# Weighing the turned states by diagonal matrices of C in a selective scan

## The chip, the cores and the metric

The kernel runs on one core of a Trainium2 chip. The metric is the device time of one execution in microseconds (us), taken as the median of repeated runs. A profile of one execution gives the time of every instruction.

## The reference

The reference is a small perceiver in float32 over 16 batches of 64 tokens with 256 channels (1024 tokens): a cross attention over 1601 context rows, a Mamba layer, a spiking feed-forward layer, a second cross attention, a self attention with a phase term, and a mixture of eight experts. The change touches the Mamba layer, whose core is this recurrence over the 64 tokens `l` of each batch (512 inner channels `d`, 16 states `n`):

```python
deltaA = jnp.exp(jnp.einsum('bld,dn->bldn', delta, a))
deltaBu = jnp.einsum('bld,bln,bld->bldn', delta, b, u)
def step(h, inp):
    dA_t, dBu_t, c_t = inp
    h = dA_t * h + dBu_t
    y = jnp.einsum('bdn,bn->bd', h, c_t)
    return (h, y)
```

The output of the scan plus `D * u` is gated by `silu(z)` and projected back to 256 channels.

## The kernel before

The Mamba stage is `mamba` (L694). Channels stand on the 128 partitions and tokens along the free axis, so the 512 channels are four blocks `c` and the 1024 tokens are two halves of 512. A unit is one token half and two channel blocks; there are four units (`UNITS`), each with 16 states, so the scan has 64 steps `s`. One step handles 128 partitions x 1024 elements (two blocks `j` of 512 tokens). Every engine runs its own list in program order, and the engines meet through semaphores. For step `s`:

- GpSimd (POOL) multiplies `du` (step size times input) by row B of state n, copied to all partitions by a transfer (`bs`, two states per transfer, three slots), into `dbu` (L847). There are three `dbu` buffers, so the product of step s waits for the scan of step s-3.
- ScalarE (ACT) makes the decays exp(-A delta) in PSUM with two instructions (`decays`, L965); it does this two steps ahead, in two buffers.
- VectorE (DVE) runs the recurrence over all 1024 elements with one scan instruction (`scan`, L1095), into three buffers `S`.
- TensorE (PE) turns the states with eight 128x128 transposes into the PSUM tile `T` (`turn`, L1174), in two halves b of four, so that tokens stand on partitions.
- The turned states are multiplied by C. Tokens are on partitions, so C is one number per partition, a column of the tile `CT`: four pieces `q` of 128x256, on ACT (`weigh`, L976), of which the last piece of 34 of the 64 steps is done by DVE (`on_dve`, L1105).
- PE turns the products back and adds them up in the PSUM tile `Y` (`add`, L1188): eight transposes against the identity.

PE's list in the loop is turn(s), then add(s-1); turn(s) waits for the scan of s and for `T` to have been emptied of step s-1. In units 1 to 3 four extra matmuls put `D * u` into `Y` (`share_of_input`, L1158). After 16 steps a unit is complete: DVE multiplies `Y` by the gate in two instructions (`gate`, L1119), which stand in DVE's list behind scan(s+1) and before scan(s+2), and PE's next add waits for them. The output projection (L1195) begins after add 62.

SyncE (SP) issues the transfers in a list of its own: late weights, the row copies of B to DRAM (`b_rows`), the `bs` loads of the first six states, then one `bs` load for every two steps, each behind a wait for POOL (L806).

Four products `du = delta * u` for the second token half are POOL's too, in front of steps 18, 22, 26 and 30 (`steps_by_input`, L826). Ahead of the loop PE turns the rows of C into `CT` (L1256) and DVE copies them (L1088).

Of the kernel before, what the change touches and what calls it, by code (L numbers as in the profile page):

```python
# [6 lines left out]
F32 = mybir.dt.float32  # L7
# [114 lines left out]
def cross_attention(nc, k, first_loads, columns, constants, loads):  # L122
# [3 lines left out]
    with ExitStack() as ctx:  # L126
# [28 lines left out]
        s_q0 = sem("a_q0")  # L155
# [370 lines left out]
        def _(e):  # L526
# [41 lines left out]
            def key_bias(f):  # L568

                ts, xs, turned = ((range(0, 1), prob[0][:, 0:D], 1), (range(1, TILES - 1), prob[1][:, 0:(TILES - 2) * D], 5),  # L570
                                  (range(TILES - 1, TILES), on[:, :], 5))[f]
                n, at = len(ts), slice(ts[0], ts[-1] + 1)
                xs = xs.rearrange("p (t d) -> p t d", d=D)
                if f == 0:
                    e.wait_ge(s_fold, 4)
                    e.tensor_copy(qconst, X[:, D:D + 1]).then_inc(s_qr, 1)
                e.wait_ge(s_t0, turned)
                e.tensor_tensor(xs, xs, X[:, 0:D].unsqueeze(1).to_broadcast([P, n, D]), ALU.mult).then_inc(s_qr, 1)
                e.wait_ge(s_qr, 2 * f + 2)
                e.reduce_sum(qraw[:, at], xs, AX.X).then_inc(s_qr, 1)  # L580
                e.wait_ge(s_qr, 2 * f + 3)
                e.tensor_scalar(qbk[:, at], qraw[:, at], qconst, scale, ALU.add, ALU.mult).then_inc(s_q0, 1)
# [9 lines left out]
            def maximum(i):  # L592
                e.wait_ge(s_sc, i + 1)
                e.reduce_max(mx[:, :], S[:, 0:LK], AX.X).then_inc(s_m1, 1)  # L594
                e.wait_ge(s_m1, i * 2 + 1)
                e.wait_ge(s_q0, 1 if i == 0 else 2 if i < TILES - 1 else 3)
# [96 lines left out]

def mamba(nc, k, m, loads):  # L694
# [11 lines left out]
    with ExitStack() as ctx:  # L706
# [4 lines left out]
        weighed = [sb(f"weighed{i}", [P, 4 * Q]) for i in range(2)]  # L711
        CT = sb("CT", [P, TILES, 2 * DS])
# [5 lines left out]
        acc4 = [weighed[r // 2][:, r % 2 * HALF:(r % 2 + 1) * HALF].rearrange("p (b l) -> p b l", l=L) for r in range(4)]  # L718
# [3 lines left out]
        qT = weighed[0][:, 0:HALF]  # L722
        kTb = k.xz[:, :, :].rearrange("p c n -> p (c n)")[:, 0:KD * (D + 1)].rearrange("p (c n) -> p c n", c=KD)
        qk, qk_at = Y.rearrange("p (j n) -> p j n", j=KD), HALF // 2 + 8
        vT, bvT = weighed[1][:, 0:HALF], weighed[1][:, HALF:HALF + KD]
# [24 lines left out]
        s_e0 = sem("n_e0")  # L750
        s_e1 = sem("n_e1")
        s_q = sem("n_q")
# [9 lines left out]
                    ("xj", 1), ("in", 12), ("dt", 1), ("in", 13), ("in", 14), ("in", 15), ("wT", 0), ("wT", 1), ("CT", 0),  # L762
# [20 lines left out]
        def on_dve(s):  # L783

            return s > 1 and s % 16 in (0, 1, 3, 5, 7, 9, 11, 13, 15)

        def dve_before(s):
            return sum(on_dve(i) for i in range(s))

        def c_of(s, q):  # L790
            return CT[:, 4 * UNITS[s // DS][0] + q, DS + s % DS:DS + s % DS + 1]

        @block.sync
        def _(e):
            loads(e)
            for h in range(2):
                if h == 0:
                    e.wait_ge(s_fa, ac_at["row", 0])
                else:
                    e.wait_ge(s_xe, 1)  # L800
                e.dma_start(m.b_dram[h], m.rows[B_AT:B_AT + DS, h * HALF:(h + 1) * HALF]).then_inc(s_bd, 16)
                e.wait_ge(s_bd, 16 * (h + 1))
                if h == 0:
                    for g in range(SLOTS):
                        load_states(e, m, g)
            for g in range(SLOTS, STEPS // 2):  # L806
                e.wait_ge(s_bu, 2 * (g - SLOTS) + 2)
                load_states(e, m, g)

        @block.gpsimd  # L810
        def _(e):
            def add_parts(c):

                e.wait_ge(s_fa, ac_at["ln", c // 2])
                e.wait_ge(s_rz, FIRST_POSITIVE.index(c) + 1)
# [3 lines left out]
            def steps_by_input(h, c):  # L819

                if h:
                    e.wait_ge(s_dl, CH)
                else:
                    e.wait_ge(s_dup, (1, 2, 5, 6)[c])
                hs = slice(h * HALF, (h + 1) * HALF)
                e.tensor_tensor(m.du[:, c, hs], m.delta[:, c, hs], m.u[:, c, hs], ALU.mult).then_inc(s_dup, 1)  # L826
# [3 lines left out]
            for c in range(2):  # L830
                steps_by_input(0, c)
            for s in range(STEPS):
                if s == 1:
                    add_parts(2)
                    add_parts(3)
                if s in (6, 10):
                    steps_by_input(0, 2 + (s - 6) // 4)
# [19 lines left out]
        def _(e):  # L857
# [145 lines left out]
            e.wait_ge(s_ct, 1)  # L1003
            for s in range(STEPS):
# [4 lines left out]
                for b in (1, 0) if on_dve(s) else (0, 1):  # L1009
                    weigh(s, b)  # L1010
# [7 lines left out]
        def _(e):  # L1018
# [68 lines left out]
            e.tensor_copy(bvT, spare[:, 0:KD])  # L1087
            e.tensor_copy(CT[:, :, :], T[:, 0:TILES * 2 * DS].rearrange("p (t n) -> p t n", n=2 * DS)).then_inc(s_ct, 1)  # L1088

# [7 lines left out]

            def weigh(s):

                e.wait_ge(s_ct, 1)  # L1100
                e.wait_ge(s_t, 2 * s + 2)
                e.wait_ge(s_e1, s + 1)
                if s >= 2:
                    e.wait_ge(s_y, 2 * (s - 2) + 2)
                e.tensor_scalar(weighed[s % 2][:, 3 * Q:4 * Q], T[:, 3 * Q:4 * Q], c_of(s, 3), None, ALU.mult  # L1105
                                ).then_inc(s_q, 1)
# [13 lines left out]

            scan(0)
# [30 lines left out]
        def _(e):  # L1152
# [9 lines left out]
            def turn(s, b):  # L1162
                if b == 0:
                    e.wait_ge(s_h, s + 1)
                    e.wait_ge(s_e0, s)
# [3 lines left out]
                else:  # L1169
                    e.wait_ge(s_e1, s)  # L1170
                    e.wait_ge(s_q, dve_before(s))
# [93 lines left out]
            e.wait_ge(s_fp, pe_at["CT", 0])  # L1265
# [1839 lines left out]
def perceiver(nc, t, out):  # L3105
    with ExitStack() as ctx:
# [9 lines left out]
        k.b_dram = nc.dram_tensor("b_rows", (2, DS, HALF), F32, kind="Internal").ap()  # L3116
        k.trig = sb("trig", [P, 2, DH])
# [14 lines left out]
        k.s_wz = sem("s_wz")  # L3132
# [13 lines left out]
        k.n_ident = k.n_const = 5 + 3 + 3 + E  # L3146
# [22 lines left out]
        def early_loads(e):  # L3169
# [10 lines left out]
            e.wait_ge(k.s_wz, 1)  # L3180
# [27 lines left out]
        def constants(e):  # L3208
# [28 lines left out]
            e.memset(k.wfq[:, :], 0.0).then_inc(k.s_wz, 1)  # L3237
# [42 lines left out]
        with ExitStack() as mctx:  # L3280
# [8 lines left out]
            m.s_bs = [sem(f"n_bs{i}") for i in range(SLOTS)]  # L3289
            mamba(nc, k, m, late_weights)  # L3290
# [75 lines left out]
```

## Time and profile before

| | |
|---|---|
| median of three runs | 658.33 us (658.2 to 660.86) |
| time of the profiled execution | 657.73 us |
| its span, first to last instruction | 656.0 us |
| the scan loop, first turn to last add | 199.9 to 364.5 us |
| busy in the span: PE, DVE, ACT, POOL | 92%, 71%, 56%, 36% |

The shares are an average over stages with different limits; the change concerns one stage, the scan loop, a quarter of the span. PE counts as busy from the start of a matmul to its modelled end, about 0.17 us after the next one may start, so the distance between starts and not the duration of one says what a matmul costs in a series. An ordinary float32 matmul appears as two matmul records, a transpose as one.

### The profile page before, as it was taken

Reading aid. Unit: us, or ns where it says so; the run is one execution under the profiler, and the core shown is the slowest. Engines: PE = TensorE matmul, PEld = TensorE weight load, DVE = VectorE, ACT = ScalarE, POOL = GpSimd, SP = SyncE. Lnnn points to the kernel's source line nnn. Section 1 sums busy time; section 2 is a strip of 40 time slices with the busy share of each in tenths; the row PEclk is TensorE's granted clock in tenths of the full one; section 3 lists DMA queues with packets and bytes.
Section 4 is the critical chain, followed back from the end, with each engine's and each line's share of the span. In section 5 each row is a group of like instructions: output and inputs, shape, how many; then the busy total and the mean of one; then the engine's idle time right before and its main releaser. Section 6 shows DMA issues by size and latency. Waiting matters only on the chain. (4 is left out here: it accounts for less than half of the span.)

```text
span 656.0 us, 11718 instructions
## 1 busy us (share of the span) xinstructions
PE 602.4 (92%) x4436; PEld 460.0 (70%) x4436; DVE 465.2 (71%) x798; ACT 368.7 (56%) x700; POOL 235.1 (36%) x190
## 2 busy tenths in 40 slices
PE   7999999999998778878788999999999899999997
PEld 6645555464366667767677888887777768889897
DVE  2753433347767999999999517788978878886554
ACT  2311111136889999999999333344656465555343
POOL 2000000000089999999898200035651022231000
PEclk8999999999999999999999999999999999999999
DMA  9999999984903232233220000000100022210001
GB/s 335 407 415 416 416 418 414 420 324 159 258 12 107 106 104 97 97 98 126 99 97 1 1 1 17 1 0 19 36 2 2 1 65 85 61 49 1 32 1 33
DMA packets 32831, 87.52 MB, mean 133 GB/s; under 512 B 8092, under 2 KB 20840, under 8 KB 30600
## 3 DMA queue, kind: packets, MB, share of 16 engines
q1 hardware_dynamic: 32088, 86.18, 35.7%
q8 instruction: 36, 0.59, 0.4%
q10 hardware_dynamic: 688, 0.59, 0.3%
q14 instruction: 19, 0.16, 0.1%
HBM read 84.53 MB, written 1.11 MB: 131 GB/s over the span
## 5 line engine op out<-in xcount | busy, mean ns | idle before, releaser
L847 POOL TENSOR_TENSOR dbu<-du,bs 128x1024 f32<-128x1024 f32 x64 | 149.8, 2365 | 7.0 <-DVE w_in L1095 4.6
L976 ACT ACTIVATE weighed<-T,CT 128x256 f32<-128x256 f32 x222 | 94.9, 592 | 1.2 <-PE T L1174 0.9
L1095 DVE TENSOR_TENSOR_SCAN w_in<-hS,dbu 128x1024 f32<-128x1024 f32 x42 | 94.6, 2271 | 0.4 <-ACT hS L965 0.4
L965 ACT ACTIVATE hS<-delta,negA 128x504 f32<-128x504 f32 x128 | 90.7, 813 | 5.3 <-DVE xn L1095 2.5
L1188 PE MATMUL Y<-ident,weighed 128*128 128x128 f32 x512 | 66.8, 273 | 0.1
L1174 PE MATMUL T<-ident,w_in 128*128 128x128 f32 x336 | 45.9, 279 | 19.8 <-ACT weighed L976 13.8
L1188 PEld LDWEIGHTS Y<-ident,weighed 128*128 128x128 f32 x512 | 57.8, 141 | 0.9 <-DVE sres L1119 0.3
L1174 PEld LDWEIGHTS T<-ident,w_in 128*128 128x128 f32 x336 | 36.1, 140 | 30.7 <-DVE w_in L1095 27.4
L1095 DVE TENSOR_TENSOR_SCAN xn<-hS,dbu 128x1024 f32<-128x1024 f32 x22 | 50.0, 2274 | 2.3 <-ACT hS L965 2.3
L425 POOL COPY w_xp<-w_xp 128x64 f32<-128x64 f32 x3 | 0.6, 234 | 138.8 <-DMA w_out<-in_w_out 138.8
L314 PE MATMUL O<-cN,pT 123*64 123x256 f32 (+1 forms) x384 | 46.7, 385 | 3.8 <-DMA cN<-in_ctx 3.1
L452 ACT ACTIVATE prob<-S,nbias 128x1601 f32<-128x1601 f32 x8 | 12.8, 1597 | 58.9 <-DVE nbias L601 58.9
L300 PE MATMUL S<-cT,qkT 128*64 128x512 f32 (+1 forms) x256 | 44.8, 502 | 0.9 <-DMA cT<-in_ctxT 0.7
L2784 ACT ACTIVATE hid<-BK,cols 128x512 f32<-128x512 f32 x32 | 22.0, 689 | 38.1 <-PE BK L2616 37.0
L3028 DVE TENSOR_TENSOR h_lo<-hid,h_hi 128x512 fp32r<-128x512 f32 x32 | 22.1, 693 | 28.6 <-ACT h_hi L2784 28.6
L314 PEld LDWEIGHTS O<-cN,pT 123*64 123x64 f32 (+1 forms) x384 | 25.4, 136 | 18.9 <-DMA cN<-in_ctx 5.0
L300 PEld LDWEIGHTS S<-cT,qkT 128*64 128x64 f32 x256 | 16.3, 136 | 30.1 <-issue 28.1
L2590 PE MATMUL BK<-w_hi,h_hi 128*128 128x256 f32 x128 | 37.1, 290 | 0.1
L594 DVE TENSOR_REDUCE mx<-S 128x1 f32<-128x1601 f32 x8 | 14.6, 1824 | 31.6 <-PE S L300 31.6
L2847 POOL TENSOR_TENSOR w_lo<-raw_w,w_hi 128x512 fp32r<-128x512 f32 x14 | 18.0, 1299 | 52.9 <-ACT w_hi L2727 52.9
L2590 PE MATMUL BK<-w_lo,h_hi 128*128 128x256 f32 x128 | 36.2, 283 | 0.0
L2590 PE MATMUL BK<-w_hi,h_lo 128*128 128x256 f32 x128 | 36.2, 283 | 0.0
(444 smaller groups left out, 1340.7 us busy)
## 6 DMA issues: line engine op xcount, KB each, us to landing
cN<-in_ctx SPq DMA_DIRECT2D x8, 3072.0 KB, 24.3
cT<-in_ctxT SPq DMA_DIRECT2D x7, 3202.0 KB, 24.5
bs<-b_rows SPq DMA_DIRECT2D x32, 512.0 KB, 3.7
raw_w<-in_w SPq DMA_DIRECT2D x16, 256.0 KB, 3.0
cT<-in_ctxT SPq DMA_DIRECT2D x1, 2178.0 KB, 12.2
cR<-in_ctx SPq DMA_DIRECT2D x8, 256.0 KB, 23.7
w<-in_w SPq DMA_DIRECT2D x7, 256.0 KB, 7.9
vs<-vx SPq DMA_DIRECT2D x8, 136.0 KB, 2.4
```

The costliest lines, as they stand in the source:

```text
L300: j = e.matmul(S[64 * b:64 * b + 64, c * HALF:c * HALF + w], qkT[:, kt, q:q + 64], cT[r][:, b, kt, c * HALF:c * HALF + w], start=kt == 0, ...
L314: j = e.matmul(O[64 * b:64 * b + 64, 0:D], pT[0:n_keys(c), c, 64 * b:64 * b + 64], v, start=c == 0, stop=c == ROWS)
L847: e.tensor_tensor(dbu[s % NB][:, :, :], half(m.du, s // DS), row, ALU.mult).then_inc(s_bu, 1)
L965: i = e.activation(by_batch(A[s % 2][:, j * HALF:(j + 1) * HALF]), by_batch(m.delta[:, c, h * HALF:(h + 1) * HALF]), ACT.Exp, scale=m.negA ...
L976: i = e.activation(weighed[s % 2][:, q * Q:(q + 1) * Q], T[:, q * Q:(q + 1) * Q], ACT.Copy, scale=c_of(s, q))
L1095: e.tensor_tensor_scan(S[s % NS], A[s % 2][:, :], dbu[s % NB][:, :, :].rearrange("p c n -> p (c n)"), 0.0, ALU.mult, ALU.add).then_inc(s_h, 1)
L1174: i = e.transpose(T[:, q * Q + j * P:q * Q + (j + 1) * P], S[s % NS][:, j * HALF + q * P:j * HALF + (q + 1) * P], k.ident[:, :])
L1188: i = e.matmul(Y[:, j * HALF + q * P:j * HALF + (q + 1) * P], weighed[s % 2][:, q * Q + j * P:q * Q + (j + 1) * P], k.ident[:, :], start=u ...
L2590: ins = e.matmul(dst, a, b, start=first and i == 0, stop=last and i == 2)
L2784: i = e.activation(dst, HB[m][:, :], ACT.Relu, bias=col(k, "b1", 2 * x + m))
L2847: e.tensor_tensor(k.w_lo[j // 2][:, j % 2, :, :], k.raw[j % SLOTS_W][:, :, :], k.w_hi[j // 2][:, j % 2, :, :].bitcast(F32), ALU.subtract). ...
L3028: e.tensor_tensor(h_lo[n % 2][:, m, :], hid[m][:, :], h_hi[n % 2][:, m, :].bitcast(F32), ALU.subtract).then_inc(s_l, 1)
```

## The change

Weighing by C moves from ACT and DVE to PE. ACT now only copies the turned states out of PSUM (two copies of 128x512 per step, `keep_turned`), DVE's part of it is gone, and `add` becomes a real float32 matmul: the copied states are the stationary operand and, in place of the identity, the moving operand is a diagonal matrix with C of that state and those 128 tokens on its diagonal. `CT`, its transposes and its copy are gone.

The diagonal matrices come from DRAM. For each token half, SP clears a 4 MB buffer from a zeroed tile, writes the 8192 values of C onto the diagonals with four transfers of 2048 elements of 4 bytes each, and loads 512 KB (two states, 128 x 2 x 512) for every two steps into three slots (`xT` halves and `xz`). For the first half all of that stands before the loop; for the second half the clearing is spread over the loop's groups 6 to 9 and the writing stands in group 12. SP's list is now, for each group g of two steps: wait and load `bs` of g; what is left of the second half's clearing or writing; wait and load the diagonals of g-1.

The four second-half products of step size and input move from POOL to DVE, behind the scans issued at steps 18, 23, 34 and 39. The two semaphores of the evacuation become one: turn(s, b) waits for copy b of step s-1, as before in substance. A few waits on constants are merged (`s_q0` into `s_qr`, `s_wz` into `s_const`).

```diff
+def clear_diagonals(e, m, h, a=0, n=DS):
+    e.dma_start(m.c_dram[h, a:a + n, 0:P * HALF].rearrange("n (p q) -> p n q", p=P),
+                m.blank.unsqueeze(1).to_broadcast([P, n, HALF])).then_inc(m.s_cd, 16)
+
+def write_diagonals(e, m, h):
+    for b in range(HALF // P):
+        diagonal = m.c_dram[h, :, b * P:b * P + P * (HALF + 1)].rearrange("n (t x) -> n t x", x=HALF + 1)[:, :, 0]
+        e.dma_start(diagonal, m.rows[C_AT:C_AT + DS, h * HALF + b * P:h * HALF + (b + 1) * P],
+                    allow_slow_non_contiguous=True).then_inc(m.s_cd, 16)
+
+def load_diagonals(e, m, g):
+    h = UNITS[2 * g // DS][0]
+    n = 2 * g % DS
+    e.dma_start(m.cd[g % SLOTS][:, :, :], m.c_dram[h, n:n + 2, 0:P * HALF].rearrange("n (p q) -> p n q", p=P)
+                ).then_inc(m.s_cl[g % SLOTS], 16)
...
@@ SyncE @@
             loads(e)
+            e.wait_ge(k.s_const, k.n_const + 1)
+            clear_diagonals(e, m, 0)
             for h in range(2):
...
                 if h == 0:
                     for g in range(SLOTS):
                         load_states(e, m, g)
-            for g in range(SLOTS, STEPS // 2):
-                e.wait_ge(s_bu, 2 * (g - SLOTS) + 2)
-                load_states(e, m, g)
+                    e.wait_ge(m.s_cd, 16)
+                    write_diagonals(e, m, 0)
+            e.wait_ge(m.s_cd, 16 * 5)
+            e.wait_ge(s_fp, pe_at["in", 15])
+            for g in range(SLOTS):
+                if g == SLOTS - 1:
+                    e.wait_ge(s_fp, pe_at["b", 0])
+                load_diagonals(e, m, g)
+            for g in range(SLOTS, STEPS // 2 + 1):
+                if g < STEPS // 2:
+                    e.wait_ge(s_bu, 2 * (g - SLOTS) + 2)
+                    load_states(e, m, g)
+                if g in range(6, 10):
+                    clear_diagonals(e, m, 1, 4 * (g - 6), 4)
+                if g == 12:
+                    e.wait_ge(m.s_cd, 16 * 9)
+                    write_diagonals(e, m, 1)
+                if g == DS + 1:
+                    e.wait_ge(m.s_cd, 16 * 13)
+                if g > SLOTS:
+                    e.wait_ge(s_y, 4 * (g - 1 - SLOTS) + 4)
+                    load_diagonals(e, m, g - 1)
...
@@ GpSimd @@
+            e.memset(m.blank, 0.0).then_inc(k.s_const, 1)
...
-                if s in (18, 22, 26, 30):
-                    steps_by_input(1, (18, 22, 26, 30).index(s))
...
@@ ScalarE @@
-            def weigh(s, b):
+            def keep_turned(s, b):
                 e.wait_ge(s_t, 2 * s + b + 1)
                 if s >= 2:
                     e.wait_ge(s_y, 2 * (s - 2) + b + 1)
-                for q in (2 * b, 2 * b + 1):
-                    if q < 3 or not on_dve(s):
-                        i = e.activation(weighed[s % 2][:, q * Q:(q + 1) * Q], T[:, q * Q:(q + 1) * Q], ACT.Copy,
-                                         scale=c_of(s, q))
-                i.then_inc((s_e0, s_e1)[b], 1)
+                e.activation(turned[s % 2][:, b * HALF:(b + 1) * HALF], T[:, b * HALF:(b + 1) * HALF], ACT.Copy
+                             ).then_inc(s_e, 1)
...
@@ VectorE @@
-            def weigh(s):
...
+            def steps_by_input(c):
+                e.wait_ge(s_dl, CH)
+                hs = slice(HALF, 2 * HALF)
+                e.tensor_tensor(m.du[:, c, hs], m.delta[:, c, hs], m.u[:, c, hs], ALU.mult).then_inc(s_dup, 1)
...
-                if on_dve(s):
-                    weigh(s)
+                if s in (18, 23, 34, 39):
+                    steps_by_input((18, 23, 34, 39).index(s))
...
@@ TensorE @@
             def add(s, b):
                 u, n = divmod(s, DS)
-                e.wait_ge((s_e0, s_e1)[b], s + 1)
-                if b and on_dve(s):
-                    e.wait_ge(s_q, dve_before(s + 1))
+                e.wait_ge(s_e, 2 * s + b + 1)
+                if b == 0:
+                    e.wait_ge(m.s_cl[s // 2 % SLOTS], 16 * (s // 2 // SLOTS + 1))
                 for j in range(2):
                     if u and n == 0 and b == 0:
                         e.wait_ge(s_yg, 2 * (u - 1) + j + 1)
                     for q in (2 * b, 2 * b + 1):
                         i = e.matmul(Y[:, j * HALF + q * P:j * HALF + (q + 1) * P],
-                                     weighed[s % 2][:, q * Q + j * P:q * Q + (j + 1) * P], k.ident[:, :],
-                                     start=u > 0 and n == 0 and q == 0, stop=True, is_transpose=True, skip_group_check=True)
+                                     turned[s % 2][:, q * Q + j * P:q * Q + (j + 1) * P],
+                                     m.cd[s // 2 % SLOTS][:, s % 2, q * P:(q + 1) * P],
+                                     start=u > 0 and n == 0 and q == 0, stop=True, skip_group_check=True)
                 i.then_inc(s_y, 1)
...
-            e.wait_ge(s_rg, 3)
-            for t in range(TILES):
-                i = e.transpose(T[:, t * 2 * DS:(t + 1) * 2 * DS], m.rows[32:64, t * P:(t + 1) * P], k.ident[32:64, 32:64])
-            i.then_inc(s_fp, 1)
```

## Rows read from the trace of the kernel before

**Rows 1.** Busy time per stretch; columns PE, PEld, DVE, ACT, POOL, clock, DMA share, GB/s

```profile
199.80:364.50 164.70, 134.17 (x1061) 116.32 (x1062) 154.41 (x102) 159.95 (x350) 154.78 (x70) 1.00 0.27 90
```

**Rows 2.** Groups of instructions by line, from 199.8 to 364.5 us

```profile
L847 POOL TENSOR_TENSOR dbu<-du,bs 128x1024 f32<-128x1024 f32 x61 | 142.8, 2365 | 6.9 <-DVE w_in L1095 4.6 <-DVE xn L1095 2.1
L976 ACT ACTIVATE weighed<-T,CT 128x256 f32<-128x256 f32 x222 | 94.9, 592 | 1.2 <-PE T L1174 0.9
L1095 DVE TENSOR_TENSOR_SCAN w_in<-hS,dbu 128x1024 f32<-128x1024 f32 x41 | 92.4, 2272 | 0.4 <-ACT hS L965 0.4
...
L1188 PE MATMUL Y<-ident,weighed 128*128 128x128 f32 x512 | 66.8, 273 | 0.1
...
L1105 DVE TENSOR_SCALAR weighed<-T,CT 128x256 f32<-128x256 f32 x34 | 16.2, 477 | 5.7 <-PE Y L1188 3.3 <-issue 0.5
...
L826 POOL TENSOR_TENSOR du<-delta,u 128x512 f32<-128x512 f32 x6 | 7.7, 1276 | 0.0
```

**Rows 3.** What ended PE's idle time before its turns (line L1174): us, times

```profile
  DVE w_in L1095: 33.9, 43
  ACT weighed L976: 22.2, 33
```

**Rows 4.** Instructions in time: turn and add of one step, then a gate

```profile
280.88 1.07 PE L1174 MATMUL T<-ident,w_in 128*128 128x128 f32 x8 [0.86 <-ACT weighed L976]
...
281.79 1.04 PE L1188 MATMUL Y<-ident,weighed 128*128 128x128 f32 x8
...
283.19 1.28 DVE L1119 TENSOR_TENSOR sres<-Y,sres 128x512 f32<-128x512 f32 x2
```

**Rows 5.** PE in time: a float32 product with 128 columns, elsewhere in the kernel

```profile
22.04 1.06 PE L273 MATMUL ptp<-xT,wq 128*128 128x128 f32 x8
```

**Rows 6.** In time: first add, two shares of input, output projection, last add

```profile
203.36 1.04 PE L1188 MATMUL Y<-ident,weighed 128*128 128x128 f32 x8
...
354.35 0.60 PE L1158 MATMUL Y<-u,diagD 128*128 128x256 f32 x2
...
361.69 1.89 PE L1195 MATMUL hS<-w_out,sres 128*128 128x256 f32 x8
...
363.42 1.04 PE L1188 MATMUL Y<-ident,weighed 128*128 128x128 f32 x8
```

**Rows 7.** In time: ACT from PSUM at 512 columns, DVE at 512, ACT's decays

```profile
173.23 2.42 ACT L896 ACTIVATE delta<-hS,cols 128x512 f32<-128x512 f32 x4
...
191.38 2.55 DVE L1051 TENSOR_TENSOR delta<-hS,delta 128x512 f32<-128x512 f32 x4 [0.40 <-ACT delta L907]
...
193.38 2.50 ACT L965 ACTIVATE hS<-delta,negA 128x504 f32<-128x504 f32 x4 [0.58 <-DVE hS L1078]
```

**Rows 8.** The page: GB/s in 40 slices of the span

```profile
GB/s 335 407 415 416 416 418 414 420 324 159 258 12 107 106 104 97 97 98 126 99 97 1 1 1 17 1 0 19 36 2 2 1 65 85 61 49 1 32 1 33
```

**Rows 9.** DMA from 168.4 to 174.2 us: the 4096 pieces of c0T, 256 bytes each

```profile
DMA packets 4248, 1.15 MB, mean 199 GB/s; under 512 B 4162, under 2 KB 4232, under 8 KB 4248
```

**Rows 10.** DMA from 183.4 to 184.1 us: the b_rows copy to DRAM

```profile
DMA packets 32, 0.03 MB, mean 47 GB/s; under 512 B 16, under 2 KB 16, under 8 KB 32
## 3 DMA queue, kind: packets, MB, share of 16 engines
q1 hardware_dynamic: 32, 0.03, 21.0%
```

**Rows 11.** The page, DMA issues: KB each, median us from issue to landing

```profile
bs<-b_rows SPq DMA_DIRECT2D x32, 512.0 KB, 3.7
...
b_rows<-xn SPq DMA_DIRECT2D x2, 32.0 KB, 2.6
```

**Rows 12.** Busy time per stretch at the kernel's start; the seventh column is PE's clock

```profile
6.00:9.40 3.40, 1.55 (x15) 1.31 (x14) 1.20 (x5) 0.52 (x1) 0.00 (x0) 1.00 1.06 391
9.40:12.80 3.40, 3.40 (x12) 2.86 (x12) 1.67 (x8) 0.73 (x4) 0.00 (x0) 0.50 1.03 411
```

More of the change, by code:

```diff
@@ L578, in key_bias @@
                 e.tensor_tensor(xs, xs, X[:, 0:D].unsqueeze(1).to_broadcast([P, n, D]), ALU.mult).then_inc(s_qr, 1)
-                e.wait_ge(s_qr, 2 * f + 2)
+                e.wait_ge(s_qr, 3 * f + 2)
                 e.reduce_sum(qraw[:, at], xs, AX.X).then_inc(s_qr, 1)
-                e.wait_ge(s_qr, 2 * f + 3)
-                e.tensor_scalar(qbk[:, at], qraw[:, at], qconst, scale, ALU.add, ALU.mult).then_inc(s_q0, 1)
+                e.wait_ge(s_qr, 3 * f + 3)
+                e.tensor_scalar(qbk[:, at], qraw[:, at], qconst, scale, ALU.add, ALU.mult).then_inc(s_qr, 1)
             def evacuate(i, g):
@@ L595, in maximum @@
                 e.wait_ge(s_m1, i * 2 + 1)
-                e.wait_ge(s_q0, 1 if i == 0 else 2 if i < TILES - 1 else 3)
+                e.wait_ge(s_qr, 4 if i == 0 else 7 if i < TILES - 1 else 10)
                 e.tensor_scalar(full_max[:, :], mx[:, :], scale, qbk[:, i:i + 1], ALU.mult, ALU.add
@@ L710, in mamba @@
         dbu = [sb(f"dbu{i}", [P, 2, HALF]) for i in range(NB)]
-        weighed = [sb(f"weighed{i}", [P, 4 * Q]) for i in range(2)]
-        CT = sb("CT", [P, TILES, 2 * DS])
+        turned = [sb(f"turned{i}", [P, 4 * Q]) for i in range(2)]
         S = [k.xn[:, 4:8, :].rearrange("p t d -> p (t d)")] + [k.w_in[:, i, :] for i in range(2)]
@@ L717, in mamba @@
         T = ps("T", [P, 2 * HALF])
-        acc4 = [weighed[r // 2][:, r % 2 * HALF:(r % 2 + 1) * HALF].rearrange("p (b l) -> p b l", l=L) for r in range(4)]
+        acc4 = [turned[r // 2][:, r % 2 * HALF:(r % 2 + 1) * HALF].rearrange("p (b l) -> p b l", l=L) for r in range(4)]
         expA = sb("expA", [P, CH * DS])
@@ L749, in mamba @@
         s_t = sem("n_t")
-        s_e0 = sem("n_e0")
-        s_e1 = sem("n_e1")
-        s_q = sem("n_q")
+        s_e = sem("n_e")
         s_y = sem("n_y")
@@ L781, in half @@
             return a[:, 2 * cp:2 * cp + 2, h * HALF:(h + 1) * HALF]
[L783 to L791, printed above, removed]
         @block.sync
@@ L817, in add_parts @@
                 e.tensor_tensor(m.delta[:, c, hs], m.delta[:, c, hs], m.du[:, c, hs], ALU.add).then_inc(s_dup, 1)
[L819 to L825, printed above, removed]
+            def steps_by_input(c):
+                e.wait_ge(s_dup, (1, 2, 5, 6)[c])
+                hs = slice(0, HALF)
                 e.tensor_tensor(m.du[:, c, hs], m.delta[:, c, hs], m.u[:, c, hs], ALU.mult).then_inc(s_dup, 1)
@@ L830, in _ @@
             for c in range(2):
-                steps_by_input(0, c)
+                steps_by_input(c)
             for s in range(STEPS):
@@ L836, in _ @@
                 if s in (6, 10):
-                    steps_by_input(0, 2 + (s - 6) // 4)
-                if s in (18, 22, 26, 30):
-                    steps_by_input(1, (18, 22, 26, 30).index(s))
+                    steps_by_input(2 + (s - 6) // 4)
                 if s % DS == 0:
@@ L1008, in _ @@
                     e.preload_act_table_set("silu_and_others")
-                for b in (1, 0) if on_dve(s) else (0, 1):
-                    weigh(s, b)
+                for b in range(2):
+                    keep_turned(s, b)
                 if s == STEPS - 2:
@@ L1086, in _ @@
             e.wait_ge(s_fp, pe_at["bv", 0])
-            e.tensor_copy(bvT, spare[:, 0:KD])
-            e.tensor_copy(CT[:, :, :], T[:, 0:TILES * 2 * DS].rearrange("p (t n) -> p t n", n=2 * DS)).then_inc(s_ct, 1)
+            e.tensor_copy(bvT, spare[:, 0:KD]).then_inc(s_ct, 1)
             def scan(s):
@@ L1168, in turn @@
                         e.wait_ge(s_vo, 2)
-                else:
-                    e.wait_ge(s_e1, s)
-                    e.wait_ge(s_q, dve_before(s))
+                if s:
+                    e.wait_ge(s_e, 2 * s - 1 + b)
                 for q in (2 * b, 2 * b + 1):
@@ L1264, in _ @@
             i.then_inc(s_fp, 1)
-            e.wait_ge(s_fp, pe_at["CT", 0])
+            e.wait_ge(s_rg, 3)
             for c in range(KD):
@@ L3116, in perceiver @@
         k.b_dram = nc.dram_tensor("b_rows", (2, DS, HALF), F32, kind="Internal").ap()
+        k.c_dram = nc.dram_tensor("c_diagonals", (2, DS, (P + 1) * HALF), F32, kind="Internal").ap()
         k.trig = sb("trig", [P, 2, DH])
@@ L3145, in perceiver @@
         k.s_d0 = sem("s_d0")
-        k.n_ident = k.n_const = 5 + 3 + 3 + E
+        k.n_const = 5 + 3 + 3 + E + 1
         k.n_w0 = 48
@@ L3179, in early_loads @@
             e.dma_start(k.trig[:, :, :], t["trig"]).then_inc(k.s_w4, 16)
-            e.wait_ge(k.s_wz, 1)
+            e.wait_ge(k.s_const, k.n_const)
             e.dma_start(k.wfq[1:3, :], t["wfq"]).then_inc(k.s_w5, 16)
@@ L3236, in constants @@
                 chain(e.memset(k.iota8[:, i:i + 1], float(i)))
-            e.memset(k.wfq[:, :], 0.0).then_inc(k.s_wz, 1)
+            chain(e.memset(k.wfq[:, :], 0.0))
         cross_attention(nc, k, first_loads, columns, constants, early_loads)
@@ L3289, in perceiver @@
             m.s_bs = [sem(f"n_bs{i}") for i in range(SLOTS)]
+            m.c_dram = k.c_dram
+            m.cd = [k.xT[:, i, :].rearrange("p (n t) -> p n t", n=2) for i in range(KD)] + [k.xz]
+            m.blank = k.gated[:, 0, :]
+            m.s_cd = sem("n_cd")
+            m.s_cl = [sem(f"n_cl{i}") for i in range(SLOTS)]
             mamba(nc, k, m, late_weights)
```

18 lines of the change are left out of this document (4 added, 14 removed).

## The prediction, made before the result

> **What bounds the kernel now.** I read the busy time of the scan stage first, then its groups by line, then what ended PE's idle time, and last single steps in order of time. The stage table says that between 199.8 and 364.5 us PE is busy for 134.2 of 164.7 us, and ACT (160.0), POOL (154.8) and DVE (154.4) more than that [rows 1]. So three engines are nearly full there and PE is the one with room. The groups give the prices: a scan 2.27 us on DVE, a product of B 2.365 us on POOL, DVE's part of the weighing 34 times 0.477 [rows 2]. A step takes 164.7 / 64 = 2.57 us. PE's idle time before its turns ends with a scan (33.9 us in 43 waits, plus those of the third scan buffer) or with a weighing by ACT (22.2 us in 33) [rows 3]: PE waits for both of the engines that the change relieves. That is what speaks for it.
>
> **PE's own price of a step.** A turn has eight records in 1.07 us and an add eight in 1.04, and the add starts 0.91 us after the turn, so there is no gap between them [rows 4]. The last record of a series stands for 0.273 us [rows 2], so starts are (1.04 - 0.273) / 7 = 0.110 us apart, and eight cost 0.877. Turn and add are 1.75 us of a step of 2.57.
>
> The change makes the add an ordinary float32 product with 128 columns. There is one like it in the trace: four products of 128x128 by 128x128 in the projection of the queries are eight records in 1.06 us [rows 5], which gives (1.06 - 0.275) / 7 = 0.112 us from start to start. The price of one record is that of a transpose; but there are two to a product. An add becomes 16 records, 1.79 us, 0.91 more than before. Nothing else in PE's loop changes, and a step then costs PE 0.877 + 1.79 = 2.67 us against a step of 2.57 now. This is the step on which the forecast hangs: the engine with room gets more than its room.
>
> **The sum for the loop.** I count from the first add (203.36) to the start of the output projection behind add 62 (361.69) [rows 6]: 158.3 us. PE's new work in that stretch: 63 adds x 1.79 = 112.6; 62 turns x 0.877 = 54.3; 12 products for the share of the input, two records each, 0.60 - 0.38 = 0.22 apart [rows 6], 5.2. Together 172.1, **+13.8 us** with no wait at all.
>
> The other engines stay below 2.67 a step. ACT: two decays, (2.50 - 0.68) / 3 = 0.61 each, and two copies of 512 columns from PSUM, (2.42 - 0.69) / 3 = 0.58 each [rows 7], 2.37. POOL: 64 x 2.365, and 2.5 for two products and 2.5 for two sums left to it [rows 2], 156.4 in all, 2.44 a step. DVE: 64 x 2.27, six gates and four products at 0.64 [rows 4, 7], 152, 2.38 a step. The move of the four products (5.1 us off POOL at 1.276 each [rows 2], 2.6 us onto DVE) and DVE's 16 us of weighing cost and give nothing, since PE hides both; without PE in the way they would give what the first rival says.
>
> **Unit boundaries.** When a unit is complete the two gates take 1.28 us [rows 4] and stand in DVE's list before the next scan. In a loop in which PE sets the pace they can't start before the last add ends, at a moment x; PE has meanwhile one turn (0.88). The gates run from x+0.2 to x+1.5, the second half of the first add waits until then, about 0.3; the scan behind the gates runs from x+1.5 to x+3.8, while PE is through with turn and add at x+3.0: a further 0.9. That is 1.2 at each of three boundaries, **+3.5**. The bounds are 0 (if the scans have run further ahead than their three buffers suggest) and 6. The product of DVE at step 18 finds the scans back to 0.3 ahead by then and costs nothing.
>
> **The tail.** Behind add 62 the projection's first part, 8 x 0.217 = 1.7, and the last add until now took 361.69 to 364.3 [rows 6], 2.6; the last add will be 1.8: 3.5, **+0.9**. The turns of C that go ahead of the loop are eight short ones beside work of ACT; I give them nothing (0 to -0.6).
>
> **The start.** The first add now also waits for the first diagonals, behind a chain on SP and the DMA queues. The small pieces of c0T are on the queues until 174.2 us [rows 9]. Behind them come 4 MB of zeros to DRAM. At the best rate of the page (415 GB/s [rows 8]) that is 10.1 us. The one write to DRAM of such pieces (2 KB) occupied the engines for 21.0% of 0.7 us for 16 pieces, one on each engine, 0.147 us a piece [rows 10], which would make 128 x 0.147 = 18.8 us. I take 14: 188.2. The copy of B's rows lies behind on the same queue and lands about 190, then three `bs` loads (3.7 us to landing [rows 11]): POOL's first product starts at about 193.5, a few us later, which the scans still bear, because the first add comes later still.
>
> Then C is written: 4 x 2048 pieces of 4 bytes, 128 of each transfer on an engine. The trace has no write of this kind. From below: the pieces of 256 bytes of c0T, 4162 small ones in 5.8 us on 16 engines [rows 9], 0.022 us each. From above: 0.147, the whole 2 KB piece to DRAM. I take 0.022, since the number of pieces and not their bytes is what the two have in common: 4 x 128 x 0.022 = 11.3 us behind the `bs` loads (drained about 194.5), so 205.8. SP waits for the landing (1.5 more) and loads the first diagonals (3.7 [rows 11], like a `bs` load in size): 211 with these, 207 with the faster clearing; I take 210. The first add starts at 210 instead of 203.4: **+6.6**. Queued on SP behind that: the `bs` load of steps 6 and 7, which POOL wants only when scan 3 is through; it lands near 212 and is hidden by PE's delay.
>
> During that wait PE stands still for 6 us. At the kernel's start PE was busy for 1.55 of 3.4 us and in the next 3.4 us had a clock of 0.50, 1.2 GHz [rows 12]. The same after this wait costs half of 3.4: **+1.5**, bounds 0 and 3. The Trainium skill (TensorE: Matmul & The Clock Gate, Part 1) states that idleness brings the clock down to half; these rows agree.
>
> The second half's C is written from group 12, in the loop. SP comes to it when add 15 is done, and stays until the load of the diagonals for step 22 can follow: 0.6 + 11.3 + 3.7, and 2.6 for the loads ahead, 18.2 us. PE needs them after seven turns, six adds, a boundary and four share products: 6.1 + 10.7 + 1.2 + 0.9 = 18.9. Hidden, with less than a us to spare. The clearings (1 MB in groups 6 to 9) and the loads (512 KB a group more) take the DMA share from 0.27 [rows 1] to some 0.6 in the loop, hidden behind 5.3 us a group.
>
> **Sum.** 13.8 + 3.5 + 0.9 + 6.6 + 1.5 = 26.3 us. The profiled execution took 657.73 (span 656.0), 0.6 below the median: 684 from it, 684.6 from the median. I say **684.5**.
>
> **Rivals.** *First, the other side: PE keeps its cover.* If an add with a diagonal costs PE no more than eight records (0.88), POOL sets the pace, with 156.4 us from its first product at 193.5 to 350; the last scan ends at 352.2, and a turn and an add later (354) the projection starts, against 361.69 now [rows 6]: 7.6 less, 651 us. It decides once an add takes less than about (158.3 - 54.3 - 5.2 - 3.5) / 63 = 1.51 us, with no wait at the start. For it speaks that ACT, DVE and POOL are all relieved; against it the eight records for four products [rows 5]. 4%.
>
> *Second, the diagonal writes are slow.* Each 0.01 us more for a piece is 5.1 us at the start and, once the 0.7 us of slack are gone, 5.1 in the loop. At 0.05: 14.3 + 13.6, 712. At the upper bound of 0.147: 64 + 63, near 811. Against it speaks only that the trace's small pieces are cheap, and they are reads from DRAM; for it that DRAM writes of 2 KB took 0.147. The Trainium skill (DMA: Bandwidth & Descriptors, Specifications) states that below 512 bytes the DMA engine reads, modifies and writes; it gives no time per piece, and no run here shows one. 30%.
>
> *Third, no wait at the start.* With faster clearing and pieces of 0.015, the diagonals land near 203: 13.8 + 3.5 + 0.9, 677. It is part of my own case, its lower half.
>
> *Fourth, no change.* The loop's extra work would have to be covered by PE waits that I count too low; the slack is 158.3 - (63 + 62) x 0.877 - 5.2 = 43.5 us and the addition 63 x 0.91 = 57.3. 3%.
>
> **Numbers.** My case (672 to 693) 63%, slow writes 30%, no change 3%, faster 4%. The range goes from 672 (no start wait, half the boundary cost) to 720 (pieces of about 0.058): it leaves out 7% below and some 11% above; my case's own range is 672 to 693. A measurement of this kernel tells 0.5% (3.3 us) from no change: faster 0.04, same 0.03, slower 0.93.
>
> **What would show it.** L1188's successor: 1024 records with starts 0.112 apart, 1.8 us an add; PE's idle time in the loop before turns nearly gone but for three places at steps 18, 34 and 50 (scan behind the gates); ACT idle 0.3 us a step, waiting for PE; POOL and DVE waiting for buffers. First add near 210, waiting for a DMA; steps then 2.67 us apart. A step below 2.5 proves the PE price wrong; a first add beyond 215, or a wait for a DMA at step 22, shows the second rival. What I trust least is the 4-byte write.

## The result, and the profile after

The changed kernel takes **695.31 us** (691.54 to 696.48, four runs), the kernel before 658.97 in the same runs: a ratio of 1.054 with an interval of 1.049 to 1.059, or 36.3 us more. The forecast was 684.5, with a range of 672 to 720. The profiled execution took 696.03, its span is 694.2 against 656.0.

The page of the changed kernel, engines first (busy us, share of the span, instructions), then two of its groups that answer to [rows 2]:

```profile
PE 655.3 (94%) x4940; PEld 526.7 (76%) x4940; DVE 457.2 (66%) x767; ACT 354.8 (51%) x606; POOL 232.8 (34%) x187
...
L1203 PE MATMUL Y<-xT,turned 128*128 128x128 f32 x704 | 87.9, 279 | 11.4 <-DMA xT<-c_diagonals 11.4
...
L1203 PE MATMUL Y<-xz,turned 128*128 128x128 f32 x320 | 40.7, 282 | 3.0 <-DMA xz<-c_diagonals 3.0
```

The add is line 1203 now, with 704 + 320 = 1024 records in place of 512. The stretches of the scan loop (busy PE, PEld, DVE, ACT, POOL, then PE's clock, DMA share, GB/s), which answer to [rows 1]:

```profile
206.20:214.70 8.50, 0.00 (x0) 0.00 (x1) 1.29 (x1) 0.00 (x0) 0.09 (x1) 0.50 0.31 109
214.70:219.80 5.10, 5.07 (x24) 5.10 (x25) 0.00 (x0) 0.43 (x1) 0.57 (x1) 0.51 0.96 335
219.80:256.40 36.60, 36.60 (x332) 36.60 (x331) 29.78 (x13) 31.30 (x56) 33.11 (x15) 1.00 0.84 296
256.40:280.90 24.50, 20.90 (x180) 20.07 (x179) 20.25 (x12) 18.16 (x33) 14.95 (x7) 1.00 0.91 120
280.90:285.30 4.40, 4.39 (x25) 4.40 (x26) 0.43 (x1) 0.26 (x1) 2.87 (x2) 0.61 1.04 408
285.30:397.40 112.10, 110.91 (x974) 109.09 (x973) 89.92 (x44) 89.92 (x159) 94.05 (x40) 1.00 0.46 163
```

Where PE has its data and its clock it is busy without a break (36.60 of 36.60 us), and DVE, ACT and POOL have become the engines with room. Before the first add it stands still for 11.4 us (8.5 of them in this table), then works at a clock of 0.51 (about 1.2 GHz of 2.4); a second, smaller hole lies before 280.9, with a clock of 0.61 behind it. The timeline of PE (start, length, instruction, and in brackets what it waited for): the first wait, two steps of the steady loop, the second wait, and the end of the loop:

```profile
214.73 3.75 PE L1203 MATMUL Y<-xT,turned 128*128 128x128 f32 x16 [11.43 <-DMA xT<-c_diagonals]
...
226.97 1.04 PE L1189 MATMUL T<-ident,w_in 128*128 128x128 f32 x8
...
227.84 1.95 PE L1203 MATMUL Y<-xz,turned 128*128 128x128 f32 x16
...
229.63 1.04 PE L1189 MATMUL T<-ident,xn 128*128 128x128 f32 x8
...
280.91 3.52 PE L1203 MATMUL Y<-xz,turned 128*128 128x128 f32 x16 [3.02 <-DMA xz<-c_diagonals]
...
397.42 1.89 PE L1211 MATMUL hS<-w_out,sres 128*128 128x256 f32 x8
...
399.15 1.95 PE L1203 MATMUL Y<-xT,turned 128*128 128x128 f32 x16
```

A step is 229.63 - 226.97 = 2.66 us; the 16 records of an add start (1.95 - 0.275) / 15 = 0.112 us apart. The first add starts at 214.73 against 203.36 [rows 6], 11.4 us later, and from there to the projection it is 182.7 us against 158.3, 24.4 more. From the starts of the adds, one by one, these 24.4 are: the PE records 13.6; three unit boundaries of 1.13 (steps of 2.82 and 3.63 in place of 2.66), 3.4; step 1, which takes 5.13 at the low clock, 2.5; steps 22 and 23 (6.28 and 4.37; in the kernel without the second writing, below, 3.10 and 2.66), 4.9. Of these 4.9, about 3.2 are the wait for diagonals (step 22) and 1.7 are the lower clock behind it (step 23, in which the add takes 3.52 us instead of 1.95). The last add costs 0.9 more. That leaves 1.5 of the 38.2 us of span, behind the loop, whose work is unchanged. It says nothing of the change: from the end of the last add to the end, the thirteen executions at hand take between 291.4 and 293.1 us, whatever the kernel (the kernel before 291.5, the changed kernel 293.1, the last run below 293.0).

### The profile page after: what moved, and what is told of

It reads as the page before. It is cut to its first block and busy times, and to the rows that moved or that the text cites. A ratio compares the mean times of both kernels' runs of the same rounds, so it can differ in the third digit from the quotient of the medians.

```text
span 694.2 us, 12538 instructions
## 1 busy us (share of the span) xinstructions
PE 655.3 (94%) x4940; PEld 526.7 (76%) x4940; DVE 457.2 (66%) x767; ACT 354.8 (51%) x606; POOL 232.8 (34%) x187
## 5 line engine op out<-in xcount | busy, mean ns | idle before, releaser
L1116 DVE TENSOR_TENSOR_SCAN w_in<-hS,dbu 128x1024 f32<-128x1024 f32 x42 | 95.4, 2281 | 30.0 <-ACT hS L991 24.4
L1203 PE MATMUL Y<-xT,turned 128*128 128x128 f32 x704 | 87.9, 279 | 11.4 <-DMA xT<-c_diagonals 11.4
L1203 PEld LDWEIGHTS Y<-xT,turned 128*128 128x128 f32 x704 | 83.9, 195 | 12.1 <-issue 12.1
L1000 ACT ACTIVATE turned<-T 128x512 f32<-128x512 f32 x128 | 69.4, 593 | 45.7 <-PE T L1189 45.6
L991 ACT ACTIVATE hS<-delta,negA 128x504 f32<-128x504 f32 x128 | 82.6, 685 | 9.3 <-DVE w_in L1116 4.8
L1189 PE MATMUL T<-ident,w_in 128*128 128x128 f32 x336 | 44.4, 276 | 1.2 <-DVE w_in L1116 1.2
L1203 PE MATMUL Y<-xz,turned 128*128 128x128 f32 x320 | 40.7, 282 | 3.0 <-DMA xz<-c_diagonals 3.0
L1203 PEld LDWEIGHTS Y<-xz,turned 128*128 128x128 f32 x320 | 38.8, 198 | 3.5 <-issue 3.4
L1189 PEld LDWEIGHTS T<-ident,w_in 128*128 128x128 f32 x336 | 39.1, 143 | 2.9 <-DVE w_in L1116 1.6
## 6 DMA issues: line engine op xcount, KB each, us to landing
c_diagonals<-gated SPq DMA_DIRECT2D x1, 4096.0 KB, 14.2
```

What stands on the lines that cost most here:

```text
L991: i = e.activation(by_batch(A[s % 2][:, j * HALF:(j + 1) * HALF]), by_batch(m.delta[:, c, h * HALF:(h + 1) * HALF]), ACT.Exp, scale=m.negA ...
L1000: e.activation(turned[s % 2][:, b * HALF:(b + 1) * HALF], T[:, b * HALF:(b + 1) * HALF], ACT.Copy).then_inc(s_e, 1)
L1116: e.tensor_tensor_scan(S[s % NS], A[s % 2][:, :], dbu[s % NB][:, :, :].rearrange("p c n -> p (c n)"), 0.0, ALU.mult, ALU.add).then_inc(s_h, 1)
L1189: i = e.transpose(T[:, q * Q + j * P:q * Q + (j + 1) * P], S[s % NS][:, j * HALF + q * P:j * HALF + (q + 1) * P], k.ident[:, :])
```

## The experiments

Theory A: PE's 16 records set the pace of the loop from the first add to the last, so what starts late is paid in full; the waits for diagonals at the start and at step 22 are queueing, and come on top. Theory B: the transfers, their order on SP and their traffic slow the loop, and the records would be hidden.

**Without the first writing (e1).**

```diff
-                    write_diagonals(e, m, 0)
```

(the counts of the waits behind it are adapted).

> The four transfers that write C of the first token half onto the diagonals are left out (these diagonals stay zero, so the first half lacks its scan part); clearing and loading stay. Changed kernel: first add at 214.8 us, step 1 takes 5.1 us, all later steps 2.66. Theory A (PE sets the pace from the first add on, so every late start is paid in full): the first diagonals land near 195, the first add moves to about 203.3 and the clock does not fall: 11.4 + 2.5 us less, 681.5 (679 to 684). Theory B (the engines behind would catch up, the start is not additive): no less than 690.

Measured: 677.42 us, ratio 1.029 (1.025 to 1.033), below the range expected. The first add moves to where it was before the change, and step 1 takes 2.66:

```profile
203.36 1.95 PE L1201 MATMUL Y<-xT,turned 128*128 128x128 f32 x16
205.15 1.04 PE L1187 MATMUL T<-ident,w_in 128*128 128x128 f32 x8
```

Theory A holds for the start. The gain is 4 us more than expected: steps 22 and 23 are down to 3.95 and 2.73 from 6.28 and 4.37, with the clock at 1.00. The second writing's pieces pass in 10.5 us in both executions, but the load behind them lands 18.5 us after SP came to the writing here (10.4 from its issue), and 20.8 us in the changed kernel (12.3 from its issue), while PE wants it after 17.9 in both. So that wait is an edge: 2.3 us on the queue decide whether PE stands still and loses its clock. Why the load landed sooner here was not found.

**Without the second writing (e2).**

```diff
-                    write_diagonals(e, m, 1)
```

(with its place in the waits).

> The four transfers in group 12 that write the second half's C are left out (the second half lacks its scan part). In the changed kernel steps 22 and 23 take 6.3 and 4.4 us in place of 2.66. Theory A (these two are waits for diagonals queued behind the writing): 5.3 us less, 690 (689 to 691.5), and steps 22 and 23 at 2.66. Theory B (they are contention of loads, not the writing): steps 22 and 23 stay long, 695.

Measured: 687.77 us, ratio 1.044 (1.042 to 1.046). Steps 22 and 23 are 3.10 (with its share of input) and 2.66: the long steps were the writing's. The total is 2 us below what was expected, just outside the range. The profiled execution shows a reason: its first add came at 211.8 instead of 214.7, and step 1 took 4.10 in place of 5.13. The first writing, the same code in both, took about 14.5 us here and 16 there; what makes it vary is not known.

**Adds as transposes, all transfers kept (e3).**

```diff
-                                     m.cd[s // 2 % SLOTS][:, s % 2, q * P:(q + 1) * P],
-                                     start=u > 0 and n == 0 and q == 0, stop=True, skip_group_check=True)
+                                     k.ident[:, :],
+                                     start=u > 0 and n == 0 and q == 0, stop=True, is_transpose=True, skip_group_check=True)
```

> The adds are transposes against the identity again (8 records), all transfers, waits and the other edits stay; nothing is weighed by C. Theory A (PE's 16 records per add are what sets the loop): first add still at 214.8, then steps near 2.4 to 2.45 set by POOL and ACT, scans made ahead are used up first: 664 (659 to 670). Theory B (the transfers, SP's order and the memory traffic slow the loop): over 680, with waits for bs or diagonals all along.

Measured: 663.34 us, ratio 1.007 (1.005 to 1.009). Most steps are 2.18 to 2.33 us (some are 1.75 to 1.8; steps 19 and 35 take 7.24 and 6.41, see the next run) although every transfer and wait of the change is there and the first add comes only at 212.0. Theory B is out: what makes the loop slow is the second record of each product. The transfers are not free in this kernel either: it takes 14.2 us more than the next one, which has none, 8.8 of them before the first add.

**No diagonals at all, adds as transposes (e7).**

```diff
-            clear_diagonals(e, m, 0)
...
-                    write_diagonals(e, m, 0)
...
-                load_diagonals(e, m, g)
```

(with their counterparts in the loop and the waits for them; the adds are changed as in the run before).

> No clearing, no writing, no loading of diagonals, adds as transposes; ACT's two plain copies and the four products on DVE stay; nothing is weighed by C. This is what the relief of ACT, DVE and POOL is worth when PE has its cover (my first rival, put at 651 with a late start, here the start is not late). Theory A: steps of 2.40 to 2.45, POOL the bound: 649 (646 to 653). Theory B (the loop before is bound by the handshake of PE and ACT, not by their work): 655 to 659.

Measured: 649.18 us, ratio 0.986 (0.984 to 0.989). This is the first rival's world, and its size is near what was put: 9.3 us below the kernel before, where the rival had 7.6. Most steps here are 2.18 or 2.33 long, which are the distances between DVE's scans and between POOL's products in a series; both are below the durations (2.27 and 2.365) by which I had counted. One step is 7.2 us long. POOL and DVE around it:

```profile
237.13 9.33 POOL L852 TENSOR_TENSOR dbu<-du,bs 128x1024 f32<-128x1024 f32 x4
249.34 2.38 POOL L852 TENSOR_TENSOR dbu<-du,bs 128x1024 f32<-128x1024 f32 x1 [2.89 <-DVE w_in L1095]
```

```profile
242.71 4.29 DVE L1115 TENSOR_TENSOR du<-delta,u 128x512 f32<-128x512 f32 x1
```

The moved product takes 4.29 us; the other three of this execution take 1.06 to 1.42, and the shortest of any run 0.66. It begins inside a series of POOL's products without a pause and ends at 247.00, 0.54 us after that series (246.46). The scans behind it wait, and PE with them for 4.0 us, behind which its clock is 0.51 from 249.2 to 252.6.

**The same with the four products back on POOL (e11).**

```diff
+                if s in (18, 22, 26, 30):
+                    steps_by_input((18, 22, 26, 30).index(s), 1)
...
-                if s in (18, 23, 34, 39):
-                    steps_by_input((18, 23, 34, 39).index(s))
```

> e7 (no diagonals, nothing weighed by C) with the four second-half products back on POOL, as in the kernel before. In e7 one of them took 4.29 us on DVE in place of 0.66, and the step behind it 7.2 us. Theory A (DVE's product with both operands in SBUF waits for a stretch of POOL's products to end, and all scans behind it): that step is gone, 5 us less, while POOL gets 5.1 us more of its own, which is the bound: 649 (647 to 651), no change in sum. Theory B (the move is worth POOL's 5 us, the 4.29 were hidden): 654.

Measured: 647.75 us, ratio 0.983 (0.982 to 0.985). The 7.2 us step is gone (the longest is 3.91) and POOL's own 5 us stand in its place: within 1.5 us of no change, as expected. Of this part the move gains nothing even where PE has room.

**The products on DVE in the kernel before (e6).**

```diff
-                if s in (18, 22, 26, 30):
-                    steps_by_input(1, (18, 22, 26, 30).index(s))
...
+                if s in (18, 23, 34, 39):
+                    steps_by_input((18, 23, 34, 39).index(s))
```

> The kernel before with one part of the change alone: the four second-half products of step size and input on DVE behind scans 19, 24, 35 and 40 instead of on POOL. Theory A (ACT with 160 of 164.7 us and its handshake with PE set the loop, POOL's 5 us are hidden): 658 to 660, no change. Theory B (POOL is the bound): 4 to 5 us less, 654.

Measured: 659.58 us, ratio 1.001 (1.000 to 1.003). No change to speak of: POOL alone was not the bound. That DVE waited long for the moved products does not hide a gain here, since they took only 0.66 to 0.96 us each.

**PE kept busy through the wait (e5).**

```diff
-                for q in (2 * b, 2 * b + 1):
+                for q in (2 * b, 2 * b + 1) * (26 if (s, b) == (1, 1) else 1):
```

> Turn 1's second half is done 26 times over (same values, one signal at the end), so that PE works for about 11 us of its wait for the first diagonals. Theory A (step 1 took 5.13 us and the first adds 3.3 instead of 1.67 because the clock had fallen to half in the wait): the granted clock stays at 1.00 there, first add still near 214.8, 2.5 us less: 692.8 (691.5 to 694). Theory B (the slow first steps are late diagonals or copies): 695 to 696, and the first steps as long as before.

Measured: 691.9 us, ratio 1.050 (1.047 to 1.053). The same two stretches as above, with PE at work in the first:

```profile
206.20:215.60 9.40, 8.80 (x81) 8.57 (x79) 0.00 (x0) 0.56 (x2) 1.04 (x1) 1.00 0.38 89
215.60:220.00 4.40, 4.37 (x39) 4.40 (x40) 2.29 (x1) 3.09 (x7) 0.00 (x0) 1.00 1.04 369
```

The clock stays at 1.00, with nothing but transposes on PE in the first stretch, and step 1 takes 2.73 in place of 5.13: 2.4 us, although the first add came 0.9 later. The slow first steps were the clock's. The Trainium skill (TensorE: Matmul & The Clock Gate, Part 1) has idleness bring the clock to half; the two executions agree.

**The same computation with the transfers in another order (e4).**

```diff
+            clear_diagonals(e, m, 0)
             loads(e)
-            clear_diagonals(e, m, 0)
...
-                if g in range(6, 10):
-                    clear_diagonals(e, m, 1, 4 * (g - 6), 4)
-                if g == 12:
-                    e.wait_ge(m.s_cd, 16 * 9)
-                    write_diagonals(e, m, 1)
+                if g in range(4, 8):
+                    clear_diagonals(e, m, 1, 4 * (g - 4), 4)
+                if g == 9:
+                    e.wait_ge(m.s_cd, 16 * 9)
+                if g in (9, 11, 13, 15):
+                    write_diagonals(e, m, 1, ((g - 9) // 2,))
+                if g in range(18, 26):
+                    k.later_weights(e, g - 18)
```

> Same computation as the changed kernel. The first clearing goes ahead of all other transfers of the stage, weights that only later stages need are loaded in groups 18 to 25, the second half's clearing comes in groups 4 to 7 and its writing one transfer at a time in groups 9, 11, 13, 15. Theory A (start and step 22 are pure queueing, PE's 2.66 a step remains): first add near 203, no long step: 676 (673 to 679). Theory B (the writing costs the same wherever it stands): at least 685.

Measured: 676.45 us, ratio 1.027 (1.025 to 1.029), as theory A has it to half a us. PE in the loop, 203 to 380 us, and one step:

```profile
203.00:380.00 177.00, 175.12 (x1538) 172.36 (x1537) 145.39 (x71) 143.33 (x252) 148.75 (x64) 1.00 0.73 227
```

```profile
240.94 1.95 PE L1206 MATMUL Y<-xT,turned 128*128 128x128 f32 x16
...
243.59 1.95 PE L1206 MATMUL Y<-xT,turned 128*128 128x128 f32 x16
```

The change as such costs 17 us and its transfers' places 19. The first writing is no faster here: its pieces pass from 179.2 to about 195, four transfers in a row as before; it ends 11 us earlier, with the clearing in front of the other loads and some of these later. Only the second writing goes one transfer at a time. Which of these moves gives how much was not tried one by one. PE is busy for 175.1 of 177.0 us, so another order of the transfers has at most 1.9 us left to give there.

**A mix of both ways (e8).** On top of the order of transfers of the run before, ACT weighs some steps by its scale as before (DVE none), the others go by diagonals.

```diff
+        def by_scale(s):
+            return s % 4 == 3
...
-                                     m.cd[s // 2 % SLOTS][:, s % 2, q * P:(q + 1) * P],
+                                     k.ident[:, :] if plain else m.cd[s // 2 % SLOTS][:, s % 2, q * P:(q + 1) * P],
```

> e4 with every fourth step weighed by ACT (four scaled pieces of 256 columns, add by transposes), the other three by diagonals. Work per step on average: PE 2.43 us, ACT 2.44, POOL 2.44, DVE 2.38. Theory A (engines' sums decide, two steps of scans ahead even them out): steps of 2.5 on average, 662 to 666 if e4 is 676. Theory B (T has one buffer, so PE and ACT cannot average over steps): a plain step costs what it cost before, 2.57, the others 2.66: 674.

Measured: 661.87 us, ratio 1.005 (1.003 to 1.007). Diagonal steps take 2.66 and scaled ones 1.75, so that a stretch of four without shares of the input is 9.73: the sums decide, 0.1 us below the range expected. PE is still the bound (160.02 of 161.80 us busy from 203 to 364.8), so more of the steps can be scaled. First six of sixteen (e10):

```diff
-            return s % 4 == 3
+            return s % DS in (2, 5, 7, 10, 12, 15)
```

> e8 with six of sixteen steps weighed by ACT (states 2, 5, 7, 10, 12, 15). PE 10 x 2.66 + 6 x 1.75 + 1.74 + 1.13 = 40.0 a unit, above ACT and POOL. Theory A: 160 us for four units, 7.2 less than e8: 654.7 (653 to 657), just below the kernel before. Theory B: no less than e8, 662 to 666.

Measured: 656.90 us, ratio 0.997 (0.995 to 0.998), within what was expected. Then every second step (e9):

```diff
-            return s % 4 == 3
+            return s % 2 == 1
```

> e8 with every second step weighed by ACT. e8's units took 12 x 2.66 + 4 x 1.75 + 1.74 (input shares) + 1.13 (boundary) = 41.8 us, PE's records throughout. With 8 and 8: PE 38.2 a unit, POOL 37.3 and its other work, ACT 8 x 2.16 + 8 x 2.64 = 38.4. Theory A (sums decide): 38.5 to 39 a unit, 13 us less than e8's loop at most, 650 to 654. Theory B (ACT and PE meet in the single buffer T in every step, so a scaled step lasts as long as ACT's 2.64 and a diagonal step 2.66): 2.65 a step, 666.

Measured: 654.50 us against 658.94, **ratio 0.993 (0.992 to 0.995), faster than both kernels**: by 0.7% of the kernel before, small but outside the noise, and half a us above the range expected. Steps alternate between 2.66 and 2.18 to 1.75; the stage table shows all four engines close together:

```profile
203.00:358.40 155.40, 149.28 (x1290) 142.69 (x1289) 143.18 (x71) 153.03 (x315) 148.23 (x65) 1.00 0.79 252
```

## Why the prediction was right, and where its sizes were off

*PE's price of a step* was the step on which all hung, and it was right: 16 records 0.112 us apart, 2.66 us a step against 2.67. It came from one row of another matmul of the same shape [rows 5]. The loop's 13.8 measured 13.6. It accounts for 17 of the 36 us: e4 shows it with the waits gone. That undoing it takes away 32 (e3) is more than its price, because an add of eight records also lets the relief of ACT, DVE and POOL through (e7 is 9 us below the kernel before) and makes up for part of the late start.

*Unit boundaries*: 1.2 each forecast, 1.13 found. *Tail*: 0.9, found 0.9. *Clock*: 1.5 forecast (half of 3.4 is 1.7), 2.5 found at the start: both halves of the add of step 0 and turn 2 fell into the stretch at 0.51, 5.1 us long. Another 1.7 came behind the wait at step 22, of which the sum had nothing.

*The start* was under-sized: +6.6 forecast, +11.4 found. The clearing was cheaper than I took it: from 172.9 to 183.6 us, 10.7 us, it ran at 398 GB/s, near the lower bound and not at 14:

```profile
DMA packets 2313, 4.25 MB, mean 398 GB/s; under 512 B 265, under 2 KB 265, under 8 KB 2313
```

The price of 0.147 us in [rows 10] was that of a small transfer and not of a piece: those rows hold 32 packets, two on each engine and half of them under 512 bytes, where I counted 16. The writing was dearer: the four transfers ran from 190.2 to 206.2 us, 16 us against 11.3. The queue's activity in those 16 us, and then to the first load of diagonals:

```profile
DMA packets 4137, 0.11 MB, mean 28 GB/s; under 512 B 4114, under 2 KB 4114, under 8 KB 4137
...
DMA packets 4103, 0.05 MB, mean 4 GB/s; under 512 B 4088, under 2 KB 4088, under 8 KB 4103
...
DMA packets 28, 0.01 MB, mean 2 GB/s; under 512 B 26, under 2 KB 26, under 8 KB 27
```

These are 190.2 to 194.2, 194.2 to 206.2 and 206.2 to 210.6 us. The first 4100 pieces take 4 us (0.016 us each on an engine), the next 4100 take 12 (0.047). And after the last piece it takes 4.4 us until the copy of the second half's B rows has landed, for which SP waits before it loads the first diagonals at 210.7; I had 1.5 for that. The two errors of size cancel, which was luck: the last piece passed at 206.2, and I had 205.8. What the start missed is the landing (2.9), a load of 4.0 in place of 3.7, and 1 us by which I had rounded my own sum of 211 down.

*The second writing* was forecast as hidden with less than a us to spare, and that failed: its pieces ran for 10.5 us (I had 11.3), but the load behind them landed 7.2 us after the last of them (12.3 from its own issue), against the 3.7 of my sum. In all 20.8 us passed from SP's coming to the writing to that landing, where I had 18.2, and PE wanted it after 17.9 and not 18.9. It stood still for 3.0 us and then lost 1.7 by its clock, 4.9 us in the two steps. The step that failed is that I took the landing of a load on a free queue for one behind a burst of small writes. With one transfer at a time, and from group 9 on (e4), no step is long. (The "four share products" of that sum are two products of two records each; the 0.9 is right.)

*The moved products* cost and gave nothing, as forecast, since PE hides them; but they are not as cheap as I had them: DVE's price of 0.64 came from an instruction with one operand in PSUM [rows 7], and the one with both in SBUF takes 0.66 to 1.42, and 4.29 three times.

*Rivals.* The first was sized well (651 against 649.2 in e7) and excluded for the right reason. The second, slow writes, came in half: the pieces cost 0.031 on average at the start and 0.021 in the loop, not 0.05; but the sign that I had set for it, a wait for a DMA at step 22, did appear.

*The whole.* The direction and the main cause were right. The 12 us by which the span grew more than the sum (38.2 against 26.3) are the start (4.8), the second writing (4.9), the first clock loss (1.0) and the 1.5 behind the loop, less 0.3. The measured 695.3 lies above my case's own range of 672 to 693, and inside the whole one because that had been kept wide for the slow writes.

## What to carry to other kernels

Before work goes to the engine with room, count its instructions in the form they will have: a float32 product is two records where a transpose is one, and 0.91 us a step against 0.69 of slack turned the engine with most room into the bound. Where a unit of work can be done in two ways that load different engines, the answer can be to alternate: half and half was 22 us better than all by diagonals with the same order of transfers (e9 against e4), and 4.4 us better than the kernel before. The other 19 of the 41 us between it and the changed kernel are the order. And place transfers with many small writes early, and loads that are needed soon not behind a burst of them: at the start the writing's own 16 us were on the path, in the loop it was the load queued behind it.

## What the runs showed of the hardware

A burst of 4-byte writes to DRAM slows down as it goes on (the two stretches of 4100 pieces above: 4 us and 12 us). By itself, in e4, a transfer of 2048 pieces passes within the 2.6 us from 244.4:

```profile
DMA packets 2060, 0.31 MB, mean 118 GB/s; under 512 B 1990, under 2 KB 1990, under 8 KB 2059
```

Four in a row took 14 to 16 us before the loop (eight executions, four with the order of e4 among them) and 9 to 10.5 us in the loop (four executions). What makes the two places differ was not tried. The Trainium skill (DMA: Bandwidth & Descriptors, Specifications) has transfers below 512 bytes read, modified and written; no run here separates that from other causes.

DVE's product of two tensors in SBUF waits for POOL's product under way, while 64 scans, which read one operand from PSUM, keep to 2.28 us beside POOL. Of 44 such products in the eleven executions that have them, 41 took 0.66 to 1.42 us. Three took 4.29 (two in e3, one in e7): they did not get in when POOL's product under way ended, but only when POOL had run out of work. The Trainium skill (SBUF — State Buffer, Who interferes with whom) states that a DVE instruction with two SBUF inputs contends with a GpSimd one that reads SBUF, since its second input comes through the read interface that the two share, and that the shared ports are an exclusive lock. The trace agrees, and adds that the wait can outlast the product under way. When it does was not found.
